# One group of gathered rows per pass moved from GpSimd's indirect DMAs to register-addressed DMAs of SyncE and ScalarE

## What is computed

```python
x = _layernorm(x + L0(x, edge_index, edge_attr_17, ...))   # one convolution gated by the edges' attributes
x = _layernorm(x + L1(x, edge_index))                      # "power": 10 times  out = 0.9 * spmm(out) + 0.1 * x
x = _layernorm(x + L2(x, edge_index))                      # "smooth": 16 times h = 0.9 * agg(norm * h) + 0.1 * x
x = _layernorm(x + L3(x, edge_index, W1, W2, ...))         # two GCN convolutions, each with a PReLU
```

## Time and profile before

| | before |
|---|---|
| median of 3 runs | 9041.95 us |
| profiled execution, its own time | 9033.9 us |
| its span (first to last instruction) | 9032.2 us |
| busy: GpSimd / TensorE / VectorE / ScalarE | 74% / 61% / 54% / 22% |
| mean granted TensorE clock | 0.647 of full speed |
| indirect DMAs of the gathers at line 1865 | 5,488, about 0.95 us each |

### The profile page before, as it was taken

One profiled execution on the slowest core, in us unless ns is written; L12 is line 12 of the kernel. 1 busy time (PEld: TensorE's weight loads), 2 busy tenths in 40 slices (PEclk: granted clock), 3 DMA queues, 4 the chain that ended last, 5 costly groups with the idle time before them and its releaser, 6 DMA issues. The chain is left out here.

```text
span 9032.2 us, 84950 instructions
## 1 busy us (share of the span) xinstructions
PE 5510.4 (61%) x23642; PEld 4389.6 (49%) x23642; DVE 4882.4 (54%) x12173; ACT 1977.5 (22%) x5359; POOL 6720.4 (74%) x7074
## 2 busy tenths in 40 slices
PE   7566544444454443347777777876676667666643
PEld 6566533333333332215666666655555556555633
DVE  7687555555565556755555555544444444465444
ACT  2355631111111111633111111100000000056433
POOL 7677677777777777677777777777777777777777
PEclk9776755555555555557777777776666676665555
DMA  8664544444444443424444444443333334333311
GB/s 145 135 180 122 94 109 105 104 104 105 105 114 107 105 101 96 134 69 106 114 109 111 111 112 112 117 103 97 96 97 96 96 96 101 95 95 89 83 45 37
DMA packets 890007, 937.80 MB, mean 104 GB/s; under 512 B 364158, under 2 KB 780032, under 8 KB 889438
## 3 DMA queue, kind: packets, MB, share of 16 engines
q1 hardware_dynamic: 646566, 587.69, 21.7%
q0 software_dynamic: 225792, 323.35, 18.8%
q10 hardware_dynamic: 17178, 21.33, 0.7%
HBM read 560.21 MB, written 399.34 MB: 106 GB/s over the span
## 5 line engine op out<-in xcount | busy, mean ns | idle before, releaser
L1865 POOL DMA_INDIRECT l_g<-tab,l x2940 | 2779.7, 945 | 909.5 <-issue 851.6
L2063 DVE TENSOR_TENSOR_SCAN l_w<-l_m,l_w,bank 96x512 f32<-96x512 bf16 x1248 | 1592.4, 1276 | 2766.2 <-PE bank L1892 2762.7
L1892 PE MATMUL bank<-ident,l_g 128*96 128x128 f32 x5096 | 1189.4, 378 | 1944.4 <-DMA l_g<-tab,l 960.6
L1865 POOL DMA_INDIRECT l_g<-tab,XM x1764 | 1671.7, 948 | 538.6 <-issue 486.5
L1892 PEld LDWEIGHTS bank<-ident,l_g 128*96 128x96 f32 x5096 | 759.6, 172 | 2409.7 <-DMA l_g<-tab,l 1077.0
L1912 PEld LDWEIGHTS bank<-ident,l_w 96*128 96x128 f32 x6272 | 1604.5, 328 | 338.3 <-issue 269.1
L1912 PE MATMUL bank<-ident,l_w 96*128 96x96 f32 x6272 | 1510.6, 404 | 9.7 <-DVE l_w L2063 9.4
L1903 PE MATMUL bank<-XM,ident 128*128 128x384 f32 x1568 | 936.5, 691 | 0.0
L1982 ACT ACTIVATE T<-T,dinv_e 128x96 f32<-128x96 f32 x196 | 57.0, 361 | 1998.9 <-DVE T L2088 1998.1
L414 ACT ACTIVATE tail_y<-bank,tail_of,tail_sc 125x96 f32<-125x96 f32 (+1 forms) x596 | 208.7, 431 | 1285.1 <-DVE tail_of L405 1285.1
L303 PE MATMUL bank<-tail_xt,v 96*96 96x500 f32 (+1 forms) x298 | 274.0, 1020 | 314.0 <-ACT tail_xt L298 314.0
(11 more groups left out here) (328 smaller groups left out, 9631.5 us busy)
## 6 DMA issues: line engine op xcount, KB each, us to landing
tab<-T SPq DMA_DIRECT2D x784, 192.0 KB, 2.4
tab<-l_o SPq DMA_DIRECT2D x441, 192.0 KB, 2.9
l_m<-mask_d SPq DMA_DIRECT2D x784, 96.0 KB, 2.8
l_m<-mask_s SPq DMA_DIRECT2D x490, 96.0 KB, 2.8
l_g<-tab,l POOLq DMA_INDIRECT x2940
l_g<-tab,XM POOLq DMA_INDIRECT x1764
x3t<-XM SPq DMA_DIRECT2D x98, 192.0 KB
x_meta<-in_x_dram SPq DMA_DIRECT2D x25, 750.0 KB
```

Source lines behind the costliest of these rows:

```text
L1865: nc.gpsimd.indirect_dma_start(out=tile(G[q % RG], t), out_offset=None, in_=tables[0:table_at + (2 - p % 2) * TR, :] if p else first, in_o ...
L1892: last = nc.tensor.transpose(a_bank(q)[0:D, u:GE:U], G[q % RG][:, u * D:(u + 1) * D], self.ident[:, :])
L2063: v.tensor_tensor_scan(out=W[q % RW][:, :], data0=masks[q % RM][:, :], data1=a_bank(q)[0:D, :], initial=W[(q - 1) % RW][:, GE - 1:GE] if q ...
```

## The change

In passes 1 to 8 of "power" and 1 to 14 of "smooth" (22 passes) group 42 (`ROW_GROUP` = 49 - 7) is no longer gathered by GpSimd, which goes from group 41 to group 43. Its 512 rows are fetched in steps 2 to 33 of the same pass: SyncE takes partitions 0 to 63, ScalarE 64 to 127, two partitions each in a step. For a partition the queue loads four indices from SBUF into four registers and issues four DMAs of one row (384 bytes) whose table address comes from a register. So each of the two queues gets 2 loads and 8 DMAs a step, 64 and 256 a pass. On SyncE they stand between the mask of group g + 4 and the store of group g - 2, on ScalarE after the background piece. Before its first row of a pass each queue waits for all stores of the pass before. The rows go into a buffer of their own (`row_buffer`) and raise two new semaphores, which TensorE waits for and clears at group 42. `full` counts the skipped groups off.

```diff
+ROW_GROUP, ROW_FROM, ROWS_EACH = NGP - 7, 2, 2
+ROW_SHARES = {"sp": (0, P // 2), "act": (P // 2, P)}
...
     def full(self, q):
 
-        return 16 * U * ((self.groups + q) // RG + 1)
+        at = self.groups + q
+        skipped = sum(k <= at and k % RG == at % RG for k in self.by_row)
+        return 16 * U * (at // RG + 1 - skipped)
...
+        self.row_buffer = sb("row_buffer", [P, GD])
+        self.rows_in = {n: self.sem(f"rows_in_{n}") for n in ("sp", "act")}
+        self.row_at = {n: [eng.alloc_register(f"row_at_{n}{u}") for u in range(U)]
+                       for n, eng in (("sp", nc.sync), ("act", nc.scalar))}
...
+        self.by_row |= {self.groups + own + p * NGP + ROW_GROUP for p in range(1, final)}
...
+            def by_rows(q):
+
+                return 1 <= q // NGP < final and q % NGP == ROW_GROUP
+
+            def fetch_rows(kind, eng, p, g):
+
+                if kind not in ROW_SHARES:
+                    return
+                begin, end = ROW_SHARES[kind]
+                n = begin + (g - ROW_FROM) * ROWS_EACH
+                if not (1 <= p < final and begin <= n < end):
+                    return
+                if n == begin:
+                    for r in range(RO):
+                        eng.wait_ge(stored[r].sem, stored[r].at + 16 * stores_before(r, p * NGP))
+                index, table = later[(p + 1) % 2], tables[0:table_at + (2 - p % 2) * TR, :]
+                for k in range(n, n + ROWS_EACH):
+                    eng.load(self.row_at[kind], index[k:k + 1, ROW_GROUP * U:(ROW_GROUP + 1) * U])
+                    for u in range(U):
+                        row = eng.snap(self.row_at[kind][u])
+                        eng.dma_start(self.row_buffer[k:k + 1, u * D:(u + 1) * D], table[bass.ds(row, 1), :]
+                                      ).then_inc(self.rows_in[kind], 16)
...
                     for g in range(NGP):
                         q = p * NGP + g
+                        if by_rows(q):
+                            continue
                         if q >= RG:
...
+                    elif by_rows(q):
+                        for n, (begin, end) in ROW_SHARES.items():
+                            pe.wait_ge(self.rows_in[n], 16 * U * (end - begin))
+                            pe.sem_clear(self.rows_in[n])
                     else:
                         landed(pe, q)
+                    rows = self.row_buffer if by_rows(q) else G[q % RG]
...
                             if g < NGP:
                                 background("act", act, p, g)
+                                fetch_rows("act", act, p, g)
                             continue
...
                         if g < NGP and p * NGP + g + RM < K * NGP:
                             load_mask(p * NGP + g + RM)
+                        fetch_rows("sp", sp, p, g)
```

More of the change, by code:

```diff
@@ L425, in __init__ @@
         self.filled = [self.sem(f"group_filled{r}") for r in range(RG)]
-        self.groups = 0
+        self.groups, self.by_row = 0, set()
     def sem(self, name):
@@ L1891, in turn @@
                     for u in range(U):
-                        last = nc.tensor.transpose(a_bank(q)[0:D, u:GE:U], G[q % RG][:, u * D:(u + 1) * D], self.ident[:, :])
+                        last = nc.tensor.transpose(a_bank(q)[0:D, u:GE:U], rows[:, u * D:(u + 1) * D], self.ident[:, :])
                     return last
```

## The result

Seven runs of the changed kernel gave 9064.08 to 9078.91 us, median 9076.7; seven of the kernel before beside them gave 9035.76 to 9046.47, median 9041.95. The ratio is 1.0037, 95% interval 1.0025 to 1.0049: slower by 0.37%, 35 us. The forecast was slower too, but by 132 us.

What follows compares the result with a forecast made beforehand. GpSimd's gathers were taken to bound every pass. Per-pass changes of +84 (smoothing with tails), -17 (without), +70 and -5 (power) summed to +132 us on 9041.95: 9174 us, range 8925 to 9800.

Steps and rivals of the forecast that it cites:

- What bounds the kernel: GpSimd's gathers set the pace in every pass at 1.248 us each; removing 88 gives at most 109.8 us.
- F: Work added to each queue per step, 2 index loads and 8 row transfers: 4.98 us, bounds 3.2 and 13.
- where it lies: Part placing F on both queues in steps 2 to 33, ahead of SyncE's store and ScalarE's next work; steps exceed 5.0 us.
- F + 5.4/6: ScalarE's need per step in smoothing passes with tails, a 5.4 us job each 6 steps: 5.88 us against 5.0.
- (9.8 + 3F)/4: Step in power passes with a job each 4 steps, three fetches having to fit into 9.8 us free: 6.19 us.
- F + 0.85: SyncE's need per step in smoothing passes without tails, F plus mask, store, gaps and waits: 5.83 us.
- The signs: Right if power steps exceed 5.5 us, roots 22, GpSimd waits for TensorE late in passes, SyncE's scan waits are gone.
- L: Lag of scan and TensorE after 32 steps: 32 x (step - 5.0) less allowed queue lateness, 4 us ScalarE, 17 SyncE.
- L - 19 - 5: Power passes' change is the larger of this and -5, GpSimd being stopped once steps are about 19 us late.
- Hidden: Rival: if F is under 4.3 all steps fit and the whole 109.8 us come, 8932 us; chance 0.40.
- In each other's way: Rival: the two queues slow each other's transfers, F 6.8, steps about 7.6, +1,260 us, 10,300 us; chance 0.11.
- edit "at nothing": Item priced at nothing: 180,000 small pieces if a row is spread over 16 engines, added to 890,007 packets.

Runs made afterwards that it cites:

- e_skip_wait40: Changed kernel, but nobody fetches group 42's rows (TensorE transposes a constant tile) and the wait before group 43 is on group 40: 8919.1 us, ratio 0.9871.
- e_act_half: Changed kernel with the wait on group 40; only ScalarE fetches its 64 partitions, SyncE none, constant tile in group 42's place: 8929.95 us, ratio 0.9876.
- e_sp_half: Changed kernel with the wait on group 40; only SyncE fetches its 64 partitions, ScalarE none, constant tile in group 42's place: 9050.05 us, ratio 1.0011.
- e_rows_only: Kernel before plus the change's whole queue work; GpSimd still gathers group 42 and TensorE uses that: 9093.34 us, ratio 1.0059.
- e_wait40: Changed kernel, but before group 43 GpSimd waits for the gathers of group 40 instead of group 41: 9044.6 us, ratio 1.0009 to the kernel before.
- e_shift: Changed kernel with the wait on group 40; SyncE fetches 52 partitions over 36 steps, ScalarE 76 over 38: 8931.49 us, ratio 0.9877.

## Why the prediction was right and wrong

- **What bounds the kernel** was right: GpSimd, 1.248 us a gather. A clean skip gave 117 us (e_skip_wait40) for the 109.8 worked out.
- **F** was right within 4 to 7%: 4.66 and 4.80 for 4.98. The load was 0.57 to 0.60 for 0.61; the transfer 0.39 to 0.43 for 0.47, its issue 0.228 where I looked for 0.34. The Trainium skill's floor of about 600 ns for such a load ("DMA: Bandwidth & Descriptors", Latency and other measured facts) is near the medians of 571 and 595 ns. As a floor this case does not bear it out: the shortest load took 460 ns.
- **The step that failed** is "where it lies", the two lines that put ScalarE's own work beside F: F + 5.4/6 a step in the smoothing passes and (9.8 + 3F)/4 in the power passes. They count the lengths of activations as time of the queue. The trace shows the queue going on under them, and e_act_half shows steps of 5.02 where the first formula, with the measured F, gives 5.70, and of 5.41 where the second gives 6.05; neither costs the pass more than 0.6 us. What costs time is SyncE (e_sp_half: 5.58 to 5.69, as slow as with both). The prediction had SyncE's sum nearly right, F + 0.85 = 5.5 with the measured F, for 5.70 measured in passes without tails, and left the tails' loads and stores out of it (5.95). I gave SyncE 17 us of allowed lateness from the masks; in passes with tails that is wrong, for a tail's load is needed two steps after its issue, and those are the waits that appear there. In passes without tails it held: 259.3 for 259.1 in e_rows_only.
- **The signs** did not tell the two queues apart. Power steps over 5.5 us (5.68), GpSimd waiting for TensorE (57.6 us) and SyncE's waits for the scan down by two thirds all came, and with SyncE as the late queue they come as well.
- **The step that was missing** is the landing wait at group 43, 2.8 to 3.5 us a pass. It was in the code beside the one that I quoted. In the passes without tails I said -2.4 and got -1.4, by two errors of opposite sign: the landing wait, which I left out, costs 3.3 of them (e_wait40), and the lag that I charged is not there (steps of 5.14 for 5.83).
- **How the two made 35 out of 132.** Power 1 to 7: forecast +10 a pass, measured +0.3. Their lag is 32 x 0.66 = 21 us, and by the prediction's own rule (L - 19 - 5) that is -3. The stall of the landing is not what is missing, for without it (e_wait40) they are no shorter. So the rule is off by 3 us there, and why stays open. Smoothing with tails: +12 forecast, +4.9 measured (L of 20 less 12 for catching up is 8). Without tails: -2.4 and -1.4. Power 8: -5 forecast, +6.3 measured; with half the jobs SyncE's queue is late all the same (5.94 us a step), and 12 own rows cover its end instead of 23, which the prediction left out. 7 x 0.3 + 6.3 + 7 x 4.9 - 7 x 1.4 = 33 us, of the 41 between the two profiled spans.
- **Luck.** With ScalarE's measured F of 4.80 in place of 4.98 the prediction's own sum gives the 9086 that it names, +44, close to the measured +35. That would have been luck: its terms are then +45 for the smoothing passes with tails, -35 without, +39 and -5 for the power passes, where +34, -10, +2 and +6 were measured.
- **The rivals.** Hidden: its rows (SyncE's 4.1 us of waiting a step) were the right ones to look at, since 4.66 into 4.1 does not go. In each other's way: e_shift has both queues at it and loses nothing, and the medians of a transfer are 228 and 226 ns with both at work. ScalarE's long first transfer behind a load, 453 ns, is as long in e_act_half, where SyncE fetches no row; so its 532 in the earlier trace rows need not be SyncE's doing. The rule of the Trainium skill ("Perfetto Trace Analysis", DMA Instruction — HWDGE) that the descriptor generator is locked by one sequencer at a time is not contradicted: at about 0.2 us a transfer 16 in 5 us need not meet much; but its price here was not to be seen.
- **Pieces of a row.** None: two packets a transfer. The 180,000 of my edit "at nothing" were 22,528.

## What to carry to other kernels

When a step is taken out of a numbered series, look at every wait that counts back by a number of steps: across the gap "two back" becomes "one back", and a wait that was always over becomes the wait for what was just issued. Work that is moved to a queue competes there with issues, register work and waits; the lengths of the engine's instructions are not simply added to it (0.25 us a step here where I had added 0.9), and a queue without an engine's work to do (SyncE) can still be the fuller one. Share such work by what each queue already issues in a step; here 52 to 76 over some more steps in place of 64 to 64, with the wait put right, turned +0.37% into -1.2%.

## What the runs showed of the hardware

- A load of four indices from SBUF into a queue's registers took 571 ns (SyncE) and 595 ns (ScalarE) in the median, and up to 2.0 us at worst.
- A row transfer of 384 bytes with a run-time address was issued in 228 ns (SyncE) and 226 (ScalarE) in the median, less than the 320 of a 128-partition store, with 44 + 29 ns of register work ahead. It made two packets. No run issues such a row in a burst at a fixed address, so what the run-time address costs in the issue itself is not shown.
- The first transfer behind an index load took 453 ns on ScalarE and 272 on SyncE in the median, the other three 220 and 228.
- ScalarE's queue issued DMAs while the engine was in its activations, and its next activation was held by those issues ("issue", 9.09 us before the one at 4863.62).
- A gather just issued by GpSimd held the next up for 3.23 us until it had landed.
